# A convolution kernel on one core: one quarter's ninth product moves into the depthwise sums' PSUM banks, and TensorE and ScalarE finish it there

## Chip, cores and metric

The kernel runs on one core of one Trainium2 chip. The metric is the device time of one execution in microseconds (us), as the median of the runs shown.

## What is computed

The input x is 32 images of 64 channels, 56 by 56, in f32. Two blocks follow each other, each on a group-normalised copy of its input (32 groups, so 2 channels to a group) and each added to its input:

```python
x = x + _L0_conv_ref(_gn(x), ...)   # sign, 3x3 depthwise with signs, PReLU, batch norm, sign, 1x1 with signs, PReLU, batch norm, + its input
x = x + _L1_conv_ref(_gn(x), W, b)  # involution

def _L1_conv_ref(x, W, b):
    filters = jnp.einsum('bchw,oc->bohw', x, W) + b[None, :, None, None]
    filters = filters.reshape(B, C, K * K, H, Wd).transpose(0, 1, 3, 4, 2)
    patches = _extract_patches(x)
    return jnp.sum(patches * filters, axis=-1)
```

The second block makes nine filters for every channel and pixel (a 1x1 convolution from 64 to 576 channels), multiplies each with one of the nine shifted copies of the normalised input, and sums the nine products. That second block is where nearly all the time goes.

## The kernel before

**Tiles and quarters.** A tile is two images, which fill the 128 partitions, so there are 16 tiles. A tile is cut into 4 quarters of 14 rows (784 pixels). A quarter has 9 units, one for each place k of the 3x3 window, so a tile has 36 units (unit 0 to unit 35) and the kernel 576.

**One unit.** TensorE makes the filter of place k with 4 matmuls of 64 by 64 in f32 (L451, `unit`); the trace shows 8 rows for them. They fill two PSUM banks of a ring of three slots, `tap_ps`. VectorE adds the bias to it and multiplies by the shifted input `q` in one instruction (L868, `product`), which frees the slot and writes a plane of `prod`. `prod` has 3 buffers of 9 planes, one buffer to a quarter.

**Summing nine planes.** A DMA issued by GpSimd adds planes 0 to 2 onto 3 to 5 (L346, `fold`). Then there are two ways:
- For quarters 1, 2 and 3 of a tile (`POOLED`, tested by `on_pool`), ScalarE adds the mean to plane 8 (L679, seen as L542, `add_mean`) and GpSimd adds planes 6 to 8 onto 3 to 5 (L364), 5 onto 3 (L374), and 3 and 4 into the output buffer `ob` (L385, `final`).
- Quarter 0 of each tile, and all four quarters of the last tile, are "kept": VectorE leaves the ninth product (k = 8) in its PSUM slot and adds it with the mean onto plane 7 in a second instruction (L882, `pair`). GpSimd adds 7 onto 6 (L355, `add_early`), 5 and 6 onto 3 and 4 (L367), and then L385.

**The first block** runs ahead of the second as 4 "jobs" a tile. A job's depthwise convolution (L486, 36 bf16 matmuls in three parts) fills `dw_ps`, a pair of PSUM banks beside the ring. ScalarE takes it out (L570 and L571, seen as L542), a pointwise matmul (L505) and a second pass (L518) use a slot of the ring with a ScalarE pass between them (relu), and VectorE adds the result to `xb` (L842, `x1_sum`), which frees the slot. The sums for the normalisations go between ScalarE (passes over 3136 elements), VectorE (shuffles, L720), GpSimd (powers, L331 and L333) and back to ScalarE, which writes `q`; SyncE copies half of it to `mirror` by DMA (L286).

**What sets the order.** Every engine runs through the same counter of units g, in program order, and waits on semaphores. Step X of a quarter stands at g = 9 x quarter + delay (`FOLD_DELAY`, `OUT_DELAY` and so on), and the steps of the first block at g = 36 x tile + place, from the tables `COURSE` and `EARLY`. So the numbers order an engine's instructions and set no time. `slots_in_turn` hands out the ring's slots and says whose release each unit waits for. VectorE's product k = 3 of a quarter waits for L385 of the quarter three before it.

The end of the last quarter is added by TensorE: `add_to_last` (L460) adds planes 0 to 5 into `dw_ps` with an identity matrix in f32:

```python
for half in range(2):
    mm = pe.matmul(dw_ps[:, half, 0:CH], ident_f32[:], prod[:, g % BUFS, k, half * CH:half * CH + CH],
                   start=(k == 0), stop=(k == PAIR_K - 3))
```

## Time and profile before

| | us |
|---|---|
| median of 3 runs | 739.9 |
| lowest and highest | 738.72, 741.68 |
| the profiled execution's own time | 737.53 |
| its span in the trace | 735.7 |
| mean granted TensorE clock, as a share of full speed | 0.977 |

The profile is of one execution. Busy time of an engine is the time in which one of its instructions ran. In a row of the timeline the first number is the start, the second the duration, both in us. Several like instructions in a row are merged (x3 and so on), and square brackets give the idle time of that engine just before, with what ended it. Consecutive instructions of VectorE overlap by some 0.08 us in these rows, so what one costs is the distance from its start to the next start. PEld is TensorE's weight load. Line numbers are those of the kernel before; all of ScalarE's activations carry the helper's line L542.

### The profile page before, as it was taken

What the parts mean: (1) busy time and instruction counts of PE and PEld (TensorE: products, weight loads), DVE (VectorE), ACT (ScalarE), POOL (GpSimd) and SP (SyncE); (2) the same over time, 40 slices, a digit from 0 to 9 for tenths busy, and PEclk for the clock granted to TensorE, in tenths of its full rate; (3) what the DMA queues carried; (4) which work ended last, traced back from release to release, by engine and by line L of the source; (5) the groups of instructions that cost most, each with busy time, mean ns of one, the idle gap of its engine ahead of it and who ended that gap; (6) DMA issues with size and microseconds to landing.
All of it is one profiled execution on the core that took longest, in us unless ns stands there. A gap on an engine that the chain in (4) does not pass through costs nothing.

```text
span 735.7 us, 18658 instructions
## 1 busy us (share of the span) xinstructions
PE 616.9 (84%) x8001; PEld 251.1 (34%) x8001; DVE 665.5 (90%) x984; ACT 501.5 (68%) x627; POOL 634.6 (86%) x330
## 2 busy tenths in 40 slices
PE   3649899897989888898888889888988889898777
PEld 2324333343333333343333334233333334332213
DVE  4839789999999998999999899999999999999885
ACT  6866896959687695959778695967769595835000
POOL 2003589999999999999999999999999999999996
PEclk9869899999999999999999999999999999999999
DMA  5235596999999798999979798989979896988874
GB/s 205 78 133 103 100 267 150 222 196 219 225 185 267 168 252 172 201 236 207 252 166 262 170 238 191 227 206 186 273 169 253 180 194 147 197 169 184 196 156 125
DMA packets 34279, 142.10 MB, mean 193 GB/s; under 512 B 3348, under 2 KB 11540, under 8 KB 32276
## 3 DMA queue, kind: packets, MB, share of 16 engines
q0 software_dynamic: 17232, 75.87, 56.0%
q1 hardware_dynamic: 16940, 65.03, 26.8%
q8 instruction: 63, 1.03, 0.5%
q14 instruction: 20, 0.16, 0.1%
q10 hardware_dynamic: 24, 0.00, 0.0%
HBM read 26.03 MB, written 25.69 MB: 70 GB/s over the span
## 4 chain that ended last, share of the span: by engine, by line
POOL 33%; DVE 22%; DMA 14%; ACT 13%; PE 12%; issue 5%; SPq 0%; POOLq 0%; DVEq 0%; ACTq 0%
DVE prod L868 16%; POOL prod L364 14%; DMA prod<-prod 11%; POOL ob L385 8%; PE tap_ps L451 7%; POOL prod L374 6%; ACT unused L542 5%; POOL prod L346 4%; DVE xb L842 3%; ACT ab L542 3%; PE dw_ps L486 3%; ACT tap_ps L542 2%; ACT st L542 2%; PE tap_ps L518 2%; DMA mirror<-q 1%
## 5 line engine op out<-in xcount | busy, mean ns | idle before, releaser
L451 PE MATMUL tap_ps<-q,w_t 64*64 64x392 f32 x2304 | 478.4, 507 | 59.6 <-DVE prod L868 38.2
L868 DVE SCALAR_TENSOR_TENSOR prod<-tap_ps,bias,q 128x784 f32<-128x784 f32 x493 | 485.3, 1026 | 31.1 <-PE tap_ps L451 19.8
L451 PE MATMUL tap_ps<-mirror,w_t 64*64 64x392 f32 x2304 | 472.7, 507 | 0.0
L451 PEld LDWEIGHTS tap_ps<-q,w_t 64*64 64x64 f32 x2304 | 147.9, 133 | 276.7 <-DVE prod L868 205.6
L364 POOL TENSOR_TENSOR prod<-prod 128x2352 f32<-128x2352 f32 x45 | 233.8, 5195 | 3.5 <-DMA prod<-prod 3.4
L542 ACT ACTIVATE ab<-dw_ps,col 128x784 bf16<-128x784 f32 x124 | 117.3, 996 | 29.7 <-PE dw_ps L486 29.7
L451 PEld LDWEIGHTS tap_ps<-mirror,w_t 64*64 64x64 f32 x2304 | 136.9, 133 | 1.1 <-issue 1.1
L486 PE MATMUL dw_ps<-signs,dw_diag 64*64 64x392 bf16 x2232 | 131.2, 336 | 6.5 <-issue 3.3
L385 POOL TENSOR_TENSOR ob<-prod 128x784 f32<-128x784 f32 x63 | 125.4, 1991 | 4.3
L346 POOL DMA_DIRECT2D prod<-prod x63 | 79.1, 1256 | 32.3 <-DVE prod L868 31.7
L374 POOL TENSOR_TENSOR prod<-prod 128x784 f32<-128x784 f32 x45 | 103.9, 2308 | 0.0
L486 PEld LDWEIGHTS dw_ps<-signs,dw_diag 64*64 64x64 bf16 x2232 | 71.1, 109 | 86.8 <-issue 75.6
L542 ACT ACTIVATE unused<-xb,st 128x3136 bf16<-128x3136 f32 x31 | 91.4, 2950 | 0.5
L542 ACT ACTIVATE tap_ps<-tap_ps,col 128x784 f32<-128x784 f32 x64 | 61.7, 965 | 39.0 <-PE tap_ps L505 39.0
L542 ACT ACTIVATE st<-st 128x1 f32<-128x1 f32 x176 | 36.4, 238 | 60.7 <-POOL st L333 47.8
L842 DVE SCALAR_TENSOR_TENSOR xb<-tap_ps,st,xb 128x784 f32<-128x784 f32 x64 | 65.9, 1030 | 11.8 <-PE tap_ps L518 10.6
L367 POOL TENSOR_TENSOR prod<-prod 128x1568 f32<-128x1568 f32 x18 | 71.1, 3949 | 0.1
L868 DVE SCALAR_TENSOR_TENSOR prod<-tap_ps,st,q 128x784 f32<-128x784 f32 x64 | 65.7, 1026 | 1.4 <-PE tap_ps L451 0.5
L542 ACT ACTIVATE q<-xb,st 128x1568 f32<-128x1568 f32 x32 | 52.6, 1693 | 0.5
L331 POOL TENSOR_SCALAR st<-st 128x1 f32<-128x1 f32 x32 | 9.4, 295 | 44.8 <-DVE st L720 43.5
L542 ACT ACTIVATE signs<-xb,st 128x3136 bf16<-128x3136 f32 (+5 forms) x20 | 47.5, 2389 | 0.5
L542 ACT ACTIVATE prod<-prod,st 128x784 f32<-128x784 f32 x45 | 42.2, 937 | 7.0 <-DVE prod L868 7.0
(118 smaller groups left out, 378.9 us busy)
## 6 DMA issues: line engine op xcount, KB each, us to landing
prod<-prod POOLq DMA_DIRECT2D x63, 1176.0 KB, 10.5
out_dram<-ob SPq DMA_DIRECT2D x31, 784.0 KB, 5.9
xb<-in_x_dram SPq DMA_DIRECT2D x15, 1568.0 KB, 10.4
mirror<-q SPq DMA_DIRECT2D x64, 203.0 KB, 5.1
xb<-in_x_dram SPq DMA_DIRECT2D x2, 784.0 KB, 5.8
out_dram<-ob SPq DMA_DIRECT2D x2, 392.0 KB, 2.4
prod<-in_L_conv_W_dram SPq DMA_DIRECT2D x1, 288.0 KB
prod<-in_L_conv_pw_weight_dram SPq DMA_DIRECT2D x1, 32.0 KB
```

What stands on the lines that cost most here:

```text
L331: pool.tensor_scalar(s_(t, var), s_(t, own), s_(t, other), EPS * N_GROUP, ALU.add, ALU.add).then_inc(var_done, 1)
L346: pool.dma_start(prod[:, g % BUFS, 3:6, :], prod[:, g % BUFS, 0:3, :], accum_op=ALU.add, max_dma_last_dim=6 * QP).then_inc(folded[g % BUFS ...
L364: pool.tensor_tensor(pr[:, 3:6, :], pr[:, 3:6, :], pr[:, 6:9, :], ALU.add).then_inc(summed_wide, 1)
L367: pool.tensor_tensor(pr[:, 3:5, :], pr[:, 3:5, :], pr[:, 5:7, :], ALU.add).then_inc(summed_wide, 1)
L374: pool.tensor_tensor(pr[3], pr[3], pr[5], ALU.add).then_inc(summed35, 1)
L385: pool.tensor_tensor(ob[:, qq, :], pr[3], pr[4], ALU.add).then_inc(summed, 1)
L451: mm = pe.matmul(rows3(tap_ps[to, slot, side, 0:CH]), w_t[own, k, :], moving, start=True, stop=True)
L486: mm = pe.matmul(rows3(banks[to, image, 0:CH]), dw_diag[own, k, own], signs[own, t.par, first:first + ROWS, dx:dx + WD], start=(k == 0), s ...
L518: mm = pe.matmul(tap_ps[to, slot, chunk, 0:CH], pw_n[own, own], ab[own, j % 2, n, image, :], start=False, stop=(n == 1), skip_group_check= ...
L542: return nc.scalar.activation(o, i, f, **kw)
L842: v.scalar_tensor_tensor(xj, tap_ps[:, slot, :, 0:CH], s_(t, RATIO), xj, ALU.mult, ALU.add, accum_out=sums[:, t.par, j:j + 1]).then_inc(x1 ...
L868: v.scalar_tensor_tensor(place.rearrange("p j (a b) -> p j a b", b=WD), psum.rearrange("p j (a b) -> p j a b", b=WD), s_(t, B4) if k == 4 ...
```

## The change

A third way to sum a quarter is added, tested by `in_banks`. It holds for quarter 3 of the tiles 0 to 14 (`SUMMED`) and for quarters 0 and 1 of the last tile (`SUMMED_LAST`). VectorE writes the ninth product into `dw_ps` instead of plane 8. TensorE adds planes 7 and 6 onto it there, by two calls of `add_in_banks` that stand at the units 10 and 11 after the quarter's first, which are units 1 and 2 of the next quarter. ScalarE takes the sum out with the mean into plane 6 (`take_from_banks`), and GpSimd goes on with L367 (5 and 6 onto 3 and 4) and L385. VectorE's `pair` and GpSimd's `add_early` are left out for these quarters. GpSimd's own way now has quarters 0, 1 and 2. Kept are only quarters 2 and 3 of the last tile. New waits guard `dw_ps`: the ninth product waits until ScalarE has emptied it (`ab_done`), and the next depthwise job waits for `take_from_banks`. The order tables are also changed, and the delays: the fold is issued two units later, `final` three.

```diff
+        def in_banks(g):
+            return g % QUARTERS in (SUMMED if g < (TILES - 1) * QUARTERS else SUMMED_LAST)
+        def is_kept(g):
+            return not on_pool(g) and not in_banks(g)
...
-                if not on_pool(g):
+                if is_kept(g):
                     pool.wait_ge(paired, kept(g))
                     pool.tensor_tensor(pr[6], pr[6], pr[7], ALU.add).then_inc(summed67, 1)
...
+            def add_in_banks(t, qq, k):
+                g = quarter(t, qq)
+                pe.wait_ge(prod_done, KK * (g + 1))
+                for half in range(2):
+                    mm = pe.matmul(dw_ps[:, half, 0:CH], ident_f32[:], prod[:, g % BUFS, k, half * CH:half * CH + CH],
+                                   start=False, stop=(k == 6), skip_group_check=True)
+                if k == 6:
+                    mm.then_inc(banks_added, 1)
...
                         wait(pe, ab_done, j - 1 if t.first else t.count(JOBS, j))
+                        wait(pe, mean_added, banks_with_mean(g))
...
+                for k, delay in ((7, BANK_DELAY), (6, BANK_DELAY + 1)):
+                    for t, qq in quarters(g, delay):
+                        if in_banks(quarter(t, qq)):
+                            add_in_banks(t, qq, k)
...
+            def take_from_banks(t, qq):
+                g = quarter(t, qq)
+                if in_banks(g):
+                    act.wait_ge(banks_added, banked(g))
+                    acts(prod[:, g % BUFS, 6, :].rearrange("p (j n) -> p j n", j=2), dw_ps[:, :, 0:CH], ACT.Identity,
+                         bias=s_(t, MEAN1)).then_inc(mean_added, 1)
...
+                elif k == PAIR_K and in_banks(g):
+                    dve.wait_ge(ab_done, convolved(g))
+                    wait(dve, mean_added, with_mean(g) - 1)
+                    place = dw_ps[:, :, 0:CH]
...
             def pair(t, qq):
                 g = quarter(t, qq)
-                if on_pool(g):
+                if not is_kept(g):
                     return
...
- 'job1': -46,
+ 'job1': -44,
...
- 'var0': -63,
+ 'var0': -65,
...
- 'inverse': -8,
+ 'inverse': -10,
...
-FOLD_DELAY = 4
+FOLD_DELAY = 6
-MEAN_DELAY = 12
+MEAN_DELAY = 10
-POOLED = 1, 2, 3
-OUT_DELAY = 25
+POOLED = 0, 1, 2
+SUMMED = 3,
+SUMMED_LAST = 0, 1
+BANK_DELAY = 10
+TAKE_DELAY = 14
+OUT_DELAY = 28
```

How the instructions move. TensorE at the start of a tile, in the changed kernel, from unit 1 of a tile in the middle (L479 is the filter matmul of `unit`, L487 the new adds; one L487 row is one matmul on one bank). In this place the kernel before has the L451 rows alone, one unit after the other.

```order
L479 MATMUL tap_ps<-q,w_t 64x392 [waits prod_done]
L479 MATMUL tap_ps<-mirror,w_t 64x392 x2
L479 MATMUL tap_ps<-q,w_t 64x392
L487 MATMUL dw_ps<-prod,ident_f 128x392 [waits prod_done]
L487 MATMUL dw_ps<-prod,ident_f 128x392
L479 MATMUL tap_ps<-q,w_t 64x392 [waits x1_done]
L479 MATMUL tap_ps<-mirror,w_t 64x392 x2
L479 MATMUL tap_ps<-q,w_t 64x392
L487 MATMUL dw_ps<-prod,ident_f 128x392 [waits prod_done]
L487 MATMUL dw_ps<-prod,ident_f 128x392
L479 MATMUL tap_ps<-q,w_t 64x392 [waits prod_done]
```

Two adds now stand between the filters of units 1 and 2 and of units 2 and 3.

GpSimd over half a tile, before: L364, L374 and L385 are one quarter's sums on GpSimd, L346 the fold's issue, L355 and L367 the kept quarter's.

```order
L331 TENSOR_SCALAR st<-st 128x1 [waits shuffled_var0]
L333 TENSOR_TENSOR st<-st,minus_half 128x1 [waits var0_done]
L364 TENSOR_TENSOR prod<-prod 128x2352 [waits mean_added,folded0]
L346 DMA prod<-prod 128x2x1176 [waits prod_done]
L374 TENSOR_TENSOR prod<-prod 128x784 [waits summed_wide]
L355 TENSOR_TENSOR prod<-prod 128x784 [waits paired]
L385 TENSOR_TENSOR ob<-prod 128x784 [waits summed35,stored1]
L367 TENSOR_TENSOR prod<-prod 128x1568 [waits summed67,folded1]
```

GpSimd in the changed kernel, in the matching stretch of a tile (L371 is the fold's issue, L395 the sum of two planes, L389 that of three, L413 `final`):

```order
L371 DMA prod<-prod 128x2x1176 [waits prod_done]
L356 TENSOR_SCALAR st<-st 128x1 [waits shuffled_var0]
L358 TENSOR_TENSOR st<-st,minus_half 128x1 [waits var0_done]
L413 TENSOR_TENSOR ob<-prod 128x784 [waits summed35,stored1]
L395 TENSOR_TENSOR prod<-prod 128x1568 [waits mean_added,folded0]
L371 DMA prod<-prod 128x2x1176 [waits prod_done]
L413 TENSOR_TENSOR ob<-prod 128x784 [waits summed_wide,stored1]
L389 TENSOR_TENSOR prod<-prod 128x2352 [waits mean_added,folded1]
```

The instruction L355 is gone, and between the issue of a quarter's fold and the first sum that needs it stand fewer instructions.

## Rows read from the trace of the kernel before

**Rows 1.** The page's first part: busy us and share of the span, by engine.

```profile
PE 616.9 (84%) x8001; PEld 251.1 (34%) x8001; DVE 665.5 (90%) x984; ACT 501.5 (68%) x627; POOL 634.6 (86%) x330
```

**Rows 2.** Timeline of VectorE over two tiles: start, us, instruction, [idle before, releaser].

```profile
485.69 1.02 DVE L868 SCALAR_TENSOR_TENSOR prod<-tap_ps,bias,q 128x784 f32<-128x784 f32 x1
486.63 1.02 DVE L882 SCALAR_TENSOR_TENSOR prod<-tap_ps,st,prod 128x784 f32<-128x784 f32 x1
487.58 0.01 DVE L720 LOAD_MASK_SELECT st<-st  x1
...
492.31 1.03 DVE L842 SCALAR_TENSOR_TENSOR xb<-tap_ps,st,xb 128x784 f32<-128x784 f32 x1 [0.65 <-PE tap_ps L518]
...
502.23 1.03 DVE L868 SCALAR_TENSOR_TENSOR prod<-tap_ps,bias,q 128x784 f32<-128x784 f32 x1 [0.94 <-POOL ob L385]
...
510.98 0.15 DVE L848 RECIPROCAL st<-st 128x1 f32<-128x1 f32 x1
...
515.40 1.03 DVE L868 SCALAR_TENSOR_TENSOR prod<-tap_ps,bias,q 128x784 f32<-128x784 f32 x1 [0.47 <-PE tap_ps L451]
...
534.19 1.03 DVE L842 SCALAR_TENSOR_TENSOR xb<-tap_ps,st,xb 128x784 f32<-128x784 f32 x1 [0.30 <-PE tap_ps L518]
...
543.64 1.03 DVE L868 SCALAR_TENSOR_TENSOR prod<-tap_ps,bias,q 128x784 f32<-128x784 f32 x1 [0.46 <-POOL ob L385]
...
550.03 1.03 DVE L842 SCALAR_TENSOR_TENSOR xb<-tap_ps,st,xb 128x784 f32<-128x784 f32 x1 [0.43 <-PE tap_ps L518]
...
552.88 0.15 DVE L848 RECIPROCAL st<-st 128x1 f32<-128x1 f32 x1
```

**Rows 3.** Timeline of GpSimd from one L367 to the next.

```profile
459.20 3.96 POOL L367 TENSOR_TENSOR prod<-prod 128x1568 f32<-128x1568 f32 x1
...
464.99 0.29 POOL L331 TENSOR_SCALAR st<-st 128x1 f32<-128x1 f32 x1 [0.67 <-DVE st L720]
...
473.35 1.24 POOL L346 DMA_DIRECT2D prod<-prod  x1 [0.43 <-DVE prod L868]
...
490.36 5.19 POOL L364 TENSOR_TENSOR prod<-prod 128x2352 f32<-128x2352 f32 x1 [0.63 <-DMA prod<-prod]
...
498.10 2.29 POOL L355 TENSOR_TENSOR prod<-prod 128x784 f32<-128x784 f32 x1
499.92 2.28 POOL L385 TENSOR_TENSOR ob<-prod 128x784 f32<-128x784 f32 x1
501.75 3.93 POOL L367 TENSOR_TENSOR prod<-prod 128x1568 f32<-128x1568 f32 x1
```

**Rows 4.** VectorE's waits: waiting line, releaser, total us, times, longest.

```profile
DVE prod L868 <- POOL ob L385: 9.8, 14, 2.2
```

**Rows 5.** Timeline of TensorE at the pair of Rows 2.

```profile
486.76 0.54 PE L451 MATMUL tap_ps<-q,w_t 64*64 64x392 f32 x1 [0.61 <-DVE prod L868]
```

**Rows 6.** Timeline of the last quarter: VectorE, and TensorE's adds into dw_ps.

```profile
717.33 2.91 DVE L868 SCALAR_TENSOR_TENSOR prod<-tap_ps,bias,q 128x784 f32<-128x784 f32 x3
...
718.28 1.58 PE L460 MATMUL dw_ps<-prod,ident_f 128*128 128x392 f32 x4
...
719.80 0.54 PE L451 MATMUL tap_ps<-q,w_t 64*64 64x392 f32 x1
...
720.62 1.58 PE L460 MATMUL dw_ps<-prod,ident_f 128*128 128x392 f32 x4
720.76 1.03 DVE L868 SCALAR_TENSOR_TENSOR prod<-tap_ps,st,q 128x784 f32<-128x784 f32 x1 [0.52 <-PE tap_ps L451]
...
723.09 1.03 DVE L868 SCALAR_TENSOR_TENSOR prod<-tap_ps,bias,q 128x784 f32<-128x784 f32 x1 [1.30 <-PE tap_ps L451]
```

**Rows 7.** Timeline of ScalarE in the first tile of Rows 2.

```profile
489.76 0.30 ACT L542 ACTIVATE st<-st 128x1 f32<-128x1 f32 x2 [2.98 <-POOL st L333]
```

**Rows 8.** Timeline of VectorE in a tile in which it never waits for GpSimd.

```profile
129.12 0.01 DVE L720 LOAD_MASK_SELECT st<-st  x1 [0.45 <-ACT unused L542]
...
130.64 1.03 DVE L842 SCALAR_TENSOR_TENSOR xb<-tap_ps,st,xb 128x784 f32<-128x784 f32 x1 [0.43 <-PE tap_ps L518]
```

**Rows 9.** Timeline of VectorE in the last tile.

```profile
709.37 1.03 DVE L868 SCALAR_TENSOR_TENSOR prod<-tap_ps,bias,q 128x784 f32<-128x784 f32 x1 [2.25 <-POOL ob L385]
```

More of the change, by code:

```diff
@@ L197, in on_pool, with banked, with_mean @@
             return g % QUARTERS in POOLED and g < (TILES - 1) * QUARTERS
+        def in_banks(g):
+            return g % QUARTERS in (SUMMED if g < (TILES - 1) * QUARTERS else SUMMED_LAST)
+        def is_kept(g):
+            return not on_pool(g) and not in_banks(g)
         def pooled(g):
             return sum(on_pool(n) for n in range(g + 1))
+        def banked(g):
+            return sum(in_banks(n) for n in range(g + 1))
         def kept(g):
-            return g + 1 - pooled(g)
+            return sum(is_kept(n) for n in range(g + 1))
+        def with_mean(g):
+            return pooled(g) + banked(g)
         def planes(g):
@@ L226, in slots_in_turn @@
                 for t, u in taps(g):
-                    if u % KK != PAIR_K or on_pool(g // KK):
+                    if u % KK != PAIR_K or not is_kept(g // KK):
                         freed["tap", g] = len(freed)
                 for t, qq in quarters(g, KK):
-                    if not on_pool(quarter(t, qq)):
+                    if is_kept(quarter(t, qq)):
                         freed["tap", KK * quarter(t, qq) + PAIR_K] = len(freed)
@@ L240, in preact_involution_kernel, with convolved, banks_with_mean @@
         slots = slots_in_turn()
+        def convolved(g):
+            return sum(1 for n in range(-2 * UNITS, KK * g + PAIR_K) for _ in jobs(n, 0))
+        def banks_with_mean(g):
+            used = [n for n in range(TILES * QUARTERS) if in_banks(n) and KK * n + BANK_DELAY <= g]
+            return with_mean(used[-1]) if used else 0
         def rows3(ap):
@@ L362, in add_wide @@
                 if on_pool(g):
-                    pool.wait_ge(mean_added, pooled(g))
+                    pool.wait_ge(mean_added, with_mean(g))
                     pool.tensor_tensor(pr[:, 3:6, :], pr[:, 3:6, :], pr[:, 6:9, :], ALU.add).then_inc(summed_wide, 1)
                 else:
-                    pool.wait_ge(summed67, kept(g))
+                    if in_banks(g):
+                        pool.wait_ge(mean_added, with_mean(g))
+                    else:
+                        pool.wait_ge(summed67, kept(g))
                     pool.tensor_tensor(pr[:, 3:5, :], pr[:, 3:5, :], pr[:, 5:7, :], ALU.add).then_inc(summed_wide, 1)
@@ L429, in wait_slot @@
                     pe.wait_ge(x1_done, n + 1)
-                elif n % KK == PAIR_K and not on_pool(n // KK):
+                elif n % KK == PAIR_K and is_kept(n // KK):
                     pe.wait_ge(paired, kept(n // KK))
@@ L457, in add_to_last @@
                 pe.wait_ge(ab_done, TILES * JOBS)
+                wait(pe, mean_added, with_mean(g))
                 pe.wait_ge(prod_done, KK * g + k + 1)
@@ L463, in add_to_last, with depthwise @@
                     mm.then_inc(last_added, 1)
-            def depthwise(t, j, taps):
+            def depthwise(t, j, taps, g):
                 if t.n < 2 and taps.start == 0:
@@ L530, in _ @@
                             add_to_last(k)
+                for k, delay in ((7, BANK_DELAY), (6, BANK_DELAY + 1)):
+                    for t, qq in quarters(g, delay):
+                        if in_banks(quarter(t, qq)):
+                            add_in_banks(t, qq, k)
                 for part in range(3):
                     for t, j in jobs(g, part):
-                        depthwise(t, j, range(3 * part, 3 * part + 3))
+                        depthwise(t, j, range(3 * part, 3 * part + 3), g)
                 for t, j in jobs(g, PW_DELAY):
@@ L683, in _ @@
                     add_mean(t, qq)
+                for t, qq in quarters(g, TAKE_DELAY):
+                    take_from_banks(t, qq)
                 for t, j in jobs(g, AB_DELAY):
@@ L866, in product @@
                 psum = tap_ps[:, slots["tap", t.count(UNITS, u)][0], :, 0:CH]
-                place = psum if k == PAIR_K and not on_pool(g) else prod[:, g % BUFS, k, :].rearrange("p (j n) -> p j n", j=2)
+                place = prod[:, g % BUFS, k, :].rearrange("p (j n) -> p j n", j=2)
+                if k == PAIR_K and is_kept(g):
+                    place = psum
+                elif k == PAIR_K and in_banks(g):
+                    dve.wait_ge(ab_done, convolved(g))
+                    wait(dve, mean_added, with_mean(g) - 1)
+                    place = dw_ps[:, :, 0:CH]
                 v.scalar_tensor_tensor(
@@ L927 @@
  'sum0': -74,
- 'mean0': -73,
+ 'mean0': -72,
  'sign0': -71,
  'square0': -67,
- 'var0': -63,
+ 'var0': -65,
  'rstd0': -65,
- 'scales0': -61,
+ 'scales0': -60,
  'inv_z': -55,
@@ L941 @@
  'mean1': -16,
- 'square1': -14,
+ 'square1': -15,
  'var1': -11,
@@ L950 @@
     0: {'sum0': -70,
-     'mean0': -100,
-     'sign0': -68,
+     'mean0': -98,
+     'sign0': -69,
      'square0': -67,
      'var0': -66,
-     'rstd0': -66,
+     'rstd0': -63,
      'scales0': -62,
      'inv_z': -60,
-     'ratio': -60,
+     'ratio': -59,
      'job0': -65,
@@ L965 @@
      'square1': -47,
-     'var1': -45,
+     'var1': -44,
      'rstd1': -49,
-     'q0': -44,
+     'q0': -47,
      'q1': -43,
-     'inverse': -44},
+     'inverse': -41},
  1: {'sum0': -100,
@@ L977 @@
      'scales0': -78,
-     'inv_z': -36,
-     'ratio': -35,
-     'job0': -37,
-     'job1': -29,
+     'inv_z': -37,
+     'ratio': -33,
+     'job0': -39,
+     'job1': -31,
      'job2': -24,
@@ L990 @@
      'q1': -7,
-     'inverse': -5},
+     'inverse': -6},
  2: {'sum0': -60,
-     'mean0': -59,
+     'mean0': -58,
      'sign0': -58,
-     'square0': -53,
-     'var0': -49,
+     'square0': -54,
+     'var0': -50,
      'rstd0': -51,
-     'scales0': -46,
+     'scales0': -47,
      'inv_z': -46,
-     'ratio': -45,
+     'ratio': -43,
      'job0': -42,
-     'job1': -37,
-     'job2': -31,
+     'job1': -32,
+     'job2': -28,
      'job3': -25},
@@ L1010 @@
  'copy_w': -45,
- 'signs_rest': -43,
- 'square_0': -57,
+ 'signs_rest': -45,
+ 'square_0': -59,
  'square_1': -53,
```

5 lines of the change are left out of this document (3 added, 2 removed).

## The prediction

> **What bounds the kernel now.** I read the page's busy times first. VectorE is busy 90% of the span, GpSimd 86%, TensorE 84%, ScalarE 68% [rows 1]. No engine is full, and two are near it, so the shares don't decide. What decides is the length of each engine's loop over one tile, against the time that a tile takes.
>
> One tile takes 41.9 us: from one reciprocal L848 to the next, 510.98 to 552.88, the distance is 41.90 us [rows 2]. GpSimd's loop comes from its timeline. From one L367 to the next are 42.55 us, of which it waited 0.67, 0.43 and 0.63 us, so its own work is 40.8 us a tile [rows 3]. VectorE's timeline over the same stretch shows products 0.94 to 0.95 us apart, and six waits in two tiles: 0.65, 0.94, 0.47, 0.30, 0.46 and 0.43 us, 3.25 together [rows 2]. Two of the six end with GpSimd's L385, and there are 14 such waits in the run, 9.8 us in all [rows 4]. Consecutive instructions overlap by about 0.08 us and a wait breaks that too, so six waits cost 3.25 + 0.48 = 3.7 us, or 1.87 us a tile. VectorE's own work is then 41.9 - 1.9 = 40.0 us. So **VectorE and GpSimd pace the kernel together**. TensorE follows VectorE through the ring: at the pair it stands idle for 0.61 us until VectorE frees a slot [rows 5]. That idle time is the slack into which the change puts work.
>
> **The change, part by part.**
>
> *Removed from VectorE:* the pair. It costs the distance to the next start, 487.58 - 486.63 = 0.95 us [rows 2]. 19 quarters had one and 2 keep it: 17 x 0.95 = 16.1 us, all on VectorE's own line.
>
> *Removed from GpSimd:* L355, 499.92 - 498.10 = 1.82 us in each of the 17 quarters [rows 3]. Its work falls from 40.8 to 39.0 us a tile. That shortens nothing by itself; it can only end VectorE's waits for L385.
>
> *Added to TensorE:* two calls of the add for each of 17 quarters. The last quarter of the kernel before makes the same call, with the same shapes, in the same alternation with filters [rows 6]. The add runs from 718.28 to the next filter's start at 719.80, so it takes 1.52 us; filter and change-over take 720.62 - 719.80 = 0.82 us; a filter is of use to VectorE 720.76 - 719.80 = 0.96 us after its first matmul. A freed slot is refilled from 1.07 us after the start of the product that frees it (486.76 against 485.69) [rows 2, 5]. With three slots VectorE comes back to a slot after 3 x 0.945 = 2.84 us, and 1.07 + 0.96 = 2.03 us are needed, so TensorE may be late by only 0.8 us.
>
> Now step by step at the start of a tile, from the start of the sum L842 that the new order places ahead of unit 0. Product 35 started at -0.95, so the filter of unit 1 starts at 0.12. The first add, which waits for that same product, runs from 0.94 to 2.46. The filter of unit 2 starts at 2.46 and is ready at 3.42. VectorE, after the sum (0.96), product 0, a shuffle (0.06) and product 1, wants it at 2.91: it waits 0.51 us. The second add runs from 3.28 to 4.80, the filter of unit 3 is ready at 5.76, and VectorE wants it at 4.37: 1.39 us. Unit 4 comes in time (6.42 for 6.71). Together **1.90 us**, 15 times: 28.5 us. The two quarters of the last tile have no sum beside them and are like the rows of the last quarter, whose waits of 0.52 and 1.30 cost 1.98 us with the overlap [rows 6]: 4.0 us. The adds cost 32.5 us in all. The bounds are nothing, if the ring hides both, and 2 x (1.52 + 0.15) = 3.3 us a place, if it hides none. I take the walk, since it repeats the waits of the rows.
>
> The row's price against a page: four matmul rows on 2 x 392 columns took 1.52 us. The Trainium skill (FP8 and Floating Point Precision, TensorE Precision Notes) has true FP32 as four passes through the array; at 2.4 GHz that is an estimate of 4 x 784 / 2.4 = 1.31 us. By it both waits shrink by 0.21 us, a place costs 1.5, and the sum ends near 740. No row bears the lower figure out.
>
> *Moved:* the relu before the pointwise's second pass now stands ahead of ScalarE's scales in its queue. Before, ScalarE sat 2.98 us until GpSimd's L333 came [rows 7], and the sum L842 behind it waited 0.65 and 0.30 us [rows 2]. I leave 0.1 of that. The waits for L385 go, since GpSimd gains 1.8 us a tile and its work between the fold that waits for product 5 and `final` is shorter by an L374. What is late next shows in a tile without such a wait: VectorE loses 0.45 us at the shuffle and 0.43 us at the sum [rows 8], with the overlap 1.04 us, as the chain of squares, shuffle and relu has its own length. The reciprocal, two units earlier, adds about 0.1. So 1.25 us of waits stay instead of 1.87: -0.62 us in each of the 12 full tiles in the middle, -7.4 us. The 2.25 us for L385 in the last tile [rows 9] go too: -2.3.
>
> *At nothing:* ScalarE's 17 new passes, one a tile, on an engine that is idle 32% of the span [rows 1]. It can start at 4.8 and the next depthwise job wants the banks at about 7.5, so it is covered unless ScalarE is in a long pass; then up to 1 us a tile shows. The ninth product into PSUM instead of SBUF: the kernel has written it to PSUM in the kept quarters all along, at the same distance.
>
> *The sum:* -16.1 + 32.5 - 7.4 - 2.3 = +6.7 us on the profiled execution's 737.5 us, 744.2. The median of the runs is 2.4 us above that execution, so **746.5 us**, slower by 0.9%.
>
> **The rivals.**
>
> *A, no change.* The pause of 1.9 us at a tile's start gives ScalarE and GpSimd time, and waits that I kept shrink by half (0.5 us in 12 tiles), or a place costs 1.5 us. For it: the chains behind them run on while VectorE stands. Against it: the chain behind the waits of 0.45 and 0.43 us begins at a sum in the middle of the tile, after the pause. 746.5 - 6 = 740.5 us.
>
> *B, faster.* The adds are hidden: TensorE is further ahead at a tile's start than the walk has it. The sum turns when a place costs under (16.1 + 7.4 + 2.3) / 17 = 1.52 us. With nothing left of it the time is 739.9 - 25.8 = 714. GpSimd's loop stops it earlier, by the mechanism of C, at about 732. I put it at 725. Against it: the add and the next filter wait for the same product, so TensorE cannot be ahead there.
>
> *C, slower than forecast.* GpSimd becomes the bound again by the fold's landing. The fold issued at 473.35 was waited for until 490.36, 17.0 us, with 16.4 us of work between [rows 3]. In the new order one L374 stands no longer between; at an L355's 1.82 us that leaves 14.6, a wait of 2.4 us. GpSimd's loop is then 39.0 + 2.4 = 41.4, with its 0.67 us for the shuffle 42.1, beside VectorE's 40.0 - 0.95 + 1.25 + 1.90 = 42.2. Two equal loops that lean on each other lose more than either: at 0.7 us a tile, 755 us. It decides if folds take over 17 us. The Trainium skill (Trainium Kernel Development and Optimization, Key Constraints) says that transfers of all queues interleave on the same 16 DMA engines; the landing just named, beside the tile's other transfers, fits.
>
> *D, the change doesn't do what it says:* excluded by the order of instructions, where L355 and the pair are gone.
>
> **How the numbers follow.** The forecast has 0.45, A 0.27, B 0.13, C 0.15. A measurement of this kernel can tell about 0.5% from no change, 736.2 to 743.6 us. B is faster, and of A 0.05: 0.18. The rest of A and 0.03 of the forecast are the same: 0.25. What is left is slower: 0.57. The range of 8 in 10 leaves out B and the upper third of C: 735 to 756. The forecast's own range is 743 to 751.
>
> **What would show it.** In the profile after, a full tile should take 42.2 us. VectorE should wait for TensorE's filter twice at each tile's start, 0.4 to 0.5 and 1.3 us, with nearly all its waits for L385 gone, and GpSimd should stand idle 2 to 3 us a tile. The adds should take 1.5 us a call. It is wrong if these two waits are missing or add up to under 1.4 us, or if VectorE still waits for GpSimd.

## The result and the profile after

The changed kernel takes **755.69 us** (median of 4 runs, 752.07 to 757.84), the kernel before 740.59 us in the same comparison. The ratio is 1.0202, with a 95% interval of 1.0153 to 1.025: it is slower by 2.0%. The forecast was 746.5 us in a range of 735 to 756. The direction held, and the range by 0.3 us; the size did not: +15 us instead of +6.6. A ratio leaves out runs that are over 1.5% above the fastest of the same kernel, which concerns only two of the four of experiment 1. The profiled execution is the one of 757.84 us, with a span of 755.9 us.

The page of the changed kernel (its busy times, the first line of its chain of waits, and two of its costliest groups; L479 is the filter matmul, L487 the new add, L371 the fold's issue):

```profile
PE 663.8 (88%) x8137; PEld 276.9 (37%) x8137; DVE 652.5 (86%) x967; ACT 519.0 (69%) x644; POOL 604.2 (80%) x313
...
PE 53%; DVE 21%; ACT 16%; DMA 6%; issue 2%; SPq 1%; POOL 1%; DVEq 0%; POOLq 0%; ACTq 0%
...
L371 POOL DMA_DIRECT2D prod<-prod x63 | 76.6, 1216 | 74.3 <-DVE prod L928 72.7
...
L487 PE MATMUL dw_ps<-prod,ident_f 128*128 128x392 f32 x136 | 54.7, 526 | 0.1
```

Against [rows 1] VectorE fell from 90% to 86% and GpSimd from 86% to 80%, while TensorE rose from 84% to 88%. Half of the chain is now TensorE's. GpSimd has spare time: it waited 72.7 us at the fold's issue for VectorE's products, where it had waited 31.7 in the kernel before (15 us of either are one wait at the start).

VectorE's waits in the changed kernel (total, times, longest one, in us; L928 is the product, L774 the shuffle, L902 the reciprocal):

```profile
DVE prod L928 <- PE tap_ps L479: 53.6, 80, 2.4
DVE st L774 <- ACT unused L586: 9.2, 14, 1.2
DVE st L902 <- ACT st L586: 8.0, 16, 1.4
```

There is no wait for GpSimd's final add left in the list, where 14 of them had cost 9.8 us [rows 4]. What stands in their place is the first line, 53.6 us for the filters. VectorE's timeline over one tile of the changed kernel says where:

```profile
358.57 1.02 DVE L896 SCALAR_TENSOR_TENSOR xb<-tap_ps,st,xb 128x784 f32<-128x784 f32 x1
...
360.54 1.02 DVE L928 SCALAR_TENSOR_TENSOR prod<-tap_ps,bias,q 128x784 f32<-128x784 f32 x1
362.01 1.03 DVE L928 SCALAR_TENSOR_TENSOR prod<-tap_ps,bias,q 128x784 f32<-128x784 f32 x1 [0.44 <-PE tap_ps L479]
364.41 1.03 DVE L928 SCALAR_TENSOR_TENSOR prod<-tap_ps,bias,q 128x784 f32<-128x784 f32 x1 [1.37 <-PE tap_ps L479]
...
374.15 1.03 DVE L928 SCALAR_TENSOR_TENSOR prod<-tap_ps,st,q 128x784 f32<-128x784 f32 x1 [0.16 <-PE tap_ps L479]
...
389.41 0.01 DVE L774 LOAD_MASK_SELECT st<-st  x1 [0.62 <-ACT unused L586]
...
390.88 0.16 DVE L902 RECIPROCAL st<-st 128x1 f32<-128x1 f32 x1 [0.38 <-ACT st L586]
```

The two waits at the tile's start, 0.44 and 1.37 us, are those of the walk (0.51 and 1.39). On TensorE's timeline the second add starts at 361.87 and the next filter at 363.38, 1.51 us later, which is the 1.52 of [rows 6]:

```profile
361.87 1.58 PE L487 MATMUL dw_ps<-prod,ident_f 128*128 128x392 f32 x4
363.38 0.54 PE L479 MATMUL tap_ps<-q,w_t 64*64 64x392 f32 x1
```

So far the mechanism is the one forecast. The length of the tiles shows what was not. From one reciprocal L902 to the next the changed kernel takes 42.01 us (348.87 to 390.88), then 43.67 (to 434.55), 42.19 (to 476.74), 43.55 (to 520.29), and so on: short tiles of 42.0 to 42.2, as forecast (42.2), and long ones of 43.6 to 44.1. TensorE's timeline where a long tile starts (its reciprocal is at 606.17; L545 and L558 are the two passes of the pointwise matmul):

```profile
603.59 0.49 PE L479 MATMUL tap_ps<-mirror,w_t 64*64 64x392 f32 x2
603.61 0.49 PE L479 MATMUL tap_ps<-q,w_t 64*64 64x392 f32 x1
605.58 0.53 PE L558 MATMUL tap_ps<-ab,pw_a_sg 64*64 64x392 bf16 x4 [1.49 <-ACT tap_ps L586]
605.89 0.55 PE L558 MATMUL tap_ps<-ab,pw_b_sg 64*64 64x392 bf16 x4
606.22 0.86 PE L479 MATMUL tap_ps<-q,w_t 64*64 64x392 f32 x1
606.22 0.86 PE L479 MATMUL tap_ps<-mirror,w_t 64*64 64x392 f32 x2
606.23 1.49 PE L479 MATMUL tap_ps<-q,w_t 64*64 64x392 f32 x2
606.88 0.86 PE L479 MATMUL tap_ps<-mirror,w_t 64*64 64x392 f32 x2
```

TensorE stood idle for 1.49 us, until ScalarE's relu let L558 start. Then matmuls of the same shape took 0.86 us in place of 0.49, and the step from one group of them to the next 0.66 in place of 0.33 (a unit has two such steps). The windows of that stretch and of the same place of the tile before, where no fall came (each starts with L558; the columns are the width and each engine's busy us, the granted clock as a share of full speed, the DMA share and GB/s):

```profile
605.60:609.10 3.50, 3.50 (x28) 1.53 (x32) 2.27 (x5) 3.13 (x6) 3.50 (x3) 0.51 1.04 184
563.60:567.10 3.50, 3.50 (x60) 1.99 (x64) 3.12 (x6) 3.12 (x6) 3.50 (x3) 1.00 1.05 185
```

The granted clock is 0.51 of full speed there, the lower of its two levels (1.2 GHz), and TensorE starts 28 matmuls in place of 60. Such stretches lie in seven full tiles of the changed kernel: from 175.6, 260.9, 305.3, 390.6, 475.9, 520.3 and 605.6 us, a little over 3 us each. Each begins between 0.3 us before and 0.7 us after the end of the idle time ahead of L558. The idle time is there in every tile, the fall only in these seven. In the kernel before no full tile in the middle has one. The spread of the changed kernel's runs goes with it roughly: 752.07 us at a mean granted clock of 0.977, 754.48 at 0.969, 756.90 at 0.964, 757.84 at 0.966.

The long tile from 305.19 takes 43.68 - 42.01 = 1.67 us more than a short one, and seven times that is 11.7 us. The profiled execution less these is 757.84 - 11.7 = 746.1 us, against the 744.2 of the sum. Of the 1.9 us that are left most are at the start of the last tile, which lies at the low clock as well (701.2 to 704.6, behind 2.48 us of idle time for the `mirror` transfer): the first add takes 2.35 us there, and VectorE waits 2.09 us for the filter behind it where other tiles have 0.44.

### The profile page after: what moved, and what is told of

Read it like the earlier page. It is cut to its first block, busy times and chain, and to the rows that moved or that the text cites. A ratio compares the mean times of both kernels' runs of the same rounds, so it can differ in the third digit from the quotient of the medians.

```text
span 755.9 us, 18972 instructions
## 1 busy us (share of the span) xinstructions
PE 663.8 (88%) x8137; PEld 276.9 (37%) x8137; DVE 652.5 (86%) x967; ACT 519.0 (69%) x644; POOL 604.2 (80%) x313
## 4 chain that ended last, share of the span: by engine, by line
PE 53%; DVE 21%; ACT 16%; DMA 6%; issue 2%; SPq 1%; POOL 1%; DVEq 0%; POOLq 0%; ACTq 0%
PE tap_ps L479 32%; DVE prod L928 15%; PE dw_ps L526 10%; PE dw_ps L487 7%; ACT unused L586 7%; DMA mirror<-q 5%; ACT ab L586 5%; DVE xb L896 3%; PE tap_ps L558 2%; ACT tap_ps L586 2%; DVE dw_ps L928 2%; ACT st L586 1%; PE dw_ps L499 1%; DMA xb<-in_x_dram 1%; PE tap_ps L545 1%
## 5 line engine op out<-in xcount | busy, mean ns | idle before, releaser
L928 DVE SCALAR_TENSOR_TENSOR prod<-tap_ps,bias,q 128x784 f32<-128x784 f32 x493 | 486.2, 1027 | 52.2 <-PE tap_ps L479 50.9
L479 PE MATMUL tap_ps<-q,w_t 64*64 64x392 f32 x2304 | 475.5, 512 | 38.0 <-DVE prod L928 20.5
L479 PE MATMUL tap_ps<-mirror,w_t 64*64 64x392 f32 x2304 | 470.9, 512 | 0.0
L389 POOL TENSOR_TENSOR prod<-prod 128x2352 f32<-128x2352 f32 x45 | 246.9, 5487 | 0.0
L479 PEld LDWEIGHTS tap_ps<-q,w_t 64*64 64x64 f32 x2304 | 152.5, 135 | 232.8 <-DVE prod L928 140.6
L479 PEld LDWEIGHTS tap_ps<-mirror,w_t 64*64 64x64 f32 x2304 | 141.8, 135 | 1.6 <-issue 1.3
L371 POOL DMA_DIRECT2D prod<-prod x63 | 76.6, 1216 | 74.3 <-DVE prod L928 72.7
L413 POOL TENSOR_TENSOR ob<-prod 128x784 f32<-128x784 f32 x63 | 133.0, 2110 | 0.1
L526 PEld LDWEIGHTS dw_ps<-signs,dw_diag 64*64 64x64 bf16 x2232 | 68.9, 110 | 96.4 <-issue 72.1
L402 POOL TENSOR_TENSOR prod<-prod 128x784 f32<-128x784 f32 x45 | 83.8, 1862 | 3.5
L928 DVE SCALAR_TENSOR_TENSOR prod<-tap_ps,st,q 128x784 f32<-128x784 f32 x64 | 65.8, 1029 | 3.0 <-PE tap_ps L479 2.6
L395 POOL TENSOR_TENSOR prod<-prod 128x1568 f32<-128x1568 f32 x18 | 65.7, 3647 | 1.7 <-DMA prod<-prod 1.6
L487 PE MATMUL dw_ps<-prod,ident_f 128*128 128x392 f32 x136 | 54.7, 526 | 0.1
```

The source lines that it names most:

```text
L371: pool.dma_start(prod[:, g % BUFS, 3:6, :], prod[:, g % BUFS, 0:3, :], accum_op=ALU.add, max_dma_last_dim=6 * QP).then_inc(folded[g % BUFS ...
L389: pool.tensor_tensor(pr[:, 3:6, :], pr[:, 3:6, :], pr[:, 6:9, :], ALU.add).then_inc(summed_wide, 1)
L395: pool.tensor_tensor(pr[:, 3:5, :], pr[:, 3:5, :], pr[:, 5:7, :], ALU.add).then_inc(summed_wide, 1)
L402: pool.tensor_tensor(pr[3], pr[3], pr[5], ALU.add).then_inc(summed35, 1)
L413: pool.tensor_tensor(ob[:, qq, :], pr[3], pr[4], ALU.add).then_inc(summed, 1)
L479: mm = pe.matmul(rows3(tap_ps[to, slot, side, 0:CH]), w_t[own, k, :], moving, start=True, stop=True)
```

## The experiments

All compare with the kernel before on the same chip: 739.3 us there in the first four, 738.2 in the next four and 738.6 in the last three. The table sums them up; "low-clock tiles" counts the full tiles between 100 and 650 us that have a stretch at half clock, in the one profiled execution of each kernel.

| kernel | us | ratio to before, 95% | low-clock tiles |
|---|---|---|---|
| the change | 755.7 | 1.020 (1.015 to 1.025) | 7 |
| 1 job 1 back | 772.6 | 1.038 (1.028 to 1.047) | 11 |
| 2 adds apart | 752.8 | 1.019 (1.015 to 1.022) | 7 |
| 3 both | 769.6 | 1.042 (1.038 to 1.045) | 9 |
| 4 adds on 8 columns | 725.0 | 0.982 (0.979 to 0.985) | 1 |
| 5 orders without adds | 742.9 | 1.006 (1.004 to 1.008) | 4 |
| 6 adds on the orders of before | 787.0 | 1.065 (1.061 to 1.068) | 3 |
| 7 job 1 back, mean later | 749.6 | 1.014 (1.010 to 1.018) | 0 |
| 8 the same, adds apart | 747.4 | 1.011 (1.007 to 1.014) | 0 |
| 9 as 7, fp16 planes | 723.5 | 0.979 (0.977 to 0.981) | 0 |
| 10 the change, fp16 planes | 723.3 | 0.979 (0.977 to 0.981) | 2 |
| 11 as 5, job 1 back, mean later | 741.1 | 1.003 (1.001 to 1.004) | 0 |

### 1. The depthwise part of job 1 where it was

In the kernel before, a depthwise part stood between the filters and L518 (the second pass of the pointwise there), where TensorE idled for 0.6 us at most in the full tiles from 170 us on:

```profile
549.38 0.36 PE L518 MATMUL tap_ps<-ab,pw_a_sg 64*64 64x392 bf16 x4 [0.43 <-ACT tap_ps L542]
```

The change moved that part two units later.

```diff
- 'job1': -44,
+ 'job1': -46,
```

> The changed kernel with one number of its order table put back: job 1 of the first block starts at -46 instead of -44, so that a part of its depthwise convolution again stands in TensorE's queue before the second pointwise pass of job 0, where TensorE of the changed kernel idles 1.49 us. Theory (half clock): in seven of the tiles of the changed kernel TensorE falls to 1.2 GHz for one stretch after that idle time, and each such tile takes 43.7 instead of 42.0 us. With the idle time filled the falls are gone from the full tiles and the median is 743 to 747 us (755.7 less 7 x 1.7). Rival (the longer tiles come from the adds or from late transfers, and the clock only goes along): every second tile stays at 43.7 us and the median is 753 to 757 us.

Measured: 772.58 us, the median of 760.99, 771.84, 773.32 and 774.58; the ratio goes by the two lower ones. A miss to the other side, by 14 us or more in every run. The trace is that of the longest run; experiment 3 has the same edit, and its four runs lie between 767.8 and 769.8. TensorE's idle times in one tile of this kernel:

```profile
353.55 0.36 PE L558 MATMUL tap_ps<-ab,pw_a_sg 64*64 64x392 bf16 x4 [0.98 <-ACT tap_ps L586]
...
360.90 0.36 PE L545 MATMUL tap_ps<-ab,pw_a 64*64 64x392 bf16 x4 [1.79 <-ACT ab L586]
...
362.51 0.54 PE L558 MATMUL tap_ps<-ab,pw_a_sg 64*64 64x392 bf16 x4 [0.42 <-ACT tap_ps L586]
```

The edit did shorten the idle time ahead of the first L558, from 1.49 to 0.98 us; that it isn't back at 0.6 has a second cause, given below with the step that failed. But job 1's own pointwise part came two units earlier too, and ScalarE wasn't ready: its timeline has the mean of quarter 2 (358.04) ahead of that job's prelu (358.88), behind 3.29 us of q. TensorE idled for 1.79 us in its place, and 0.42 more ahead of L558, and there the clock fell (granted clock 0.51 from 362.3 to 365.7), now in nearly every full tile: tiles of 44.4 us. Eleven full tiles had a fall, where the change had seven. The remedy moved the idle time and made it longer. The link from idle time to low clock stood; that the adds or the load do it was as open as before.

### 2. The adds apart

```diff
-                for k, delay in ((7, BANK_DELAY), (6, BANK_DELAY + 1)):
+                for k, delay in ((7, BANK_DELAY), (6, BANK_DELAY + 3)):
```

> The changed kernel with the second add two units later: plane 6 at unit 4 of the next quarter instead of unit 2. Theory (ring slack): an add alone makes TensorE 1.5 us late, of which the ring hides 0.8 us, and two in neighbouring units find the slack gone. Apart, VectorE waits about 0.5 us for each instead of 0.44 and 1.37 us: 17 x 0.85 = 14 us less, a median of 740 to 744 us while the falls of the clock stay. Rival (TensorE is full at a tile's start, so that the wait only moves): waits of 0.4 and 1.3 us as before at another unit, 753 to 757 us.

Measured: 752.83 us, 2.9 less than the change. A miss: it lies by the rival's 753 to 757 us, and the waits came as neither had them. VectorE's timeline at a tile's start:

```profile
405.16 1.98 DVE L928 SCALAR_TENSOR_TENSOR prod<-tap_ps,bias,q 128x784 f32<-128x784 f32 x2 [0.59 <-PE tap_ps L479]
...
408.81 2.92 DVE L928 SCALAR_TENSOR_TENSOR prod<-tap_ps,bias,q 128x784 f32<-128x784 f32 x3 [0.73 <-PE tap_ps L479]
```

The wait for the second add fell from 1.37 to 0.73 us, but the one before it grew to 0.59 and another later in the tile from 0.16 to 0.27. Between the two adds TensorE can't catch up: VectorE takes a product each 0.95 us, and a filter with its add takes more than two of them. Seven tiles kept their fall of the clock.

### 3. Both

> Both edits: job 1 at -46 and the second add at unit 4. Theory (ring slack and half clock, two costs that add up): 755.7 - 12 - 14, a median of 728 to 732 us, 1.2% faster than the kernel before. Rival (GpSimd's loop over a tile with the fold's landing, about 42 us, is the next bound): the gains do not add up, no less than 739 us, and VectorE waits for L385's counterpart again.

Measured: 769.59 us, the edits of 1 and 2 together. A miss for the reason of the first: TensorE idles for 1.77 us ahead of job 1's L545 in every full tile, and nine of them had a fall. What the adds apart give here isn't clear, since the runs of the first lie between 761.0 and 774.6.

### 4. Adds on eight columns

The two planes are added on 8 of 392 columns, so most of them is left out of the sum; every instruction and wait stays.

```diff
-                    mm = pe.matmul(dw_ps[:, half, 0:CH], ident_f32[:], prod[:, g % BUFS, k, half * CH:half * CH + CH],
+                    mm = pe.matmul(dw_ps[:, half, 0:8], ident_f32[:], prod[:, g % BUFS, k, half * CH:half * CH + 8],
```

> The changed kernel with every add cut to 8 columns of each bank; all waits and semaphores stay. Left out: planes 6 and 7 are added on 8 of 392 columns only. Theory (ring slack): the two waits at a tile's start vanish, 17 x 1.9 = 32 us less, a median of 722 to 728 us, and the falls of the clock stay in every second tile. Rival (GpSimd's loop takes over, as it was the other pacer before): 738 to 742 us with VectorE waiting for GpSimd.

Measured: 725.03 us, a hit: 30.7 us less than the change, where the prediction put the adds at 32.5. VectorE waited 17.4 us for filters in place of 53.6:

```profile
DVE prod L928 <- PE tap_ps L479: 17.4, 29, 2.4
```

Its waits for GpSimd's final add were 1.3 us in 7 times. So GpSimd is hardly a bound even 30 us lower, and rival C has no place.

But the 30.7 us are not the adds alone. One full tile had the low clock here and seven in the change, and at 1.67 us a tile that is an estimate of 10 of them. A full tile without the low clock takes 40.65 us (338.89 to 379.54) against the change's 42.01, so the adds cost 1.36 us a tile, less than the 1.97 us of their waits. The rest is in waits that only this kernel's tiles have:

```profile
357.65 0.01 DVE L774 LOAD_MASK_SELECT st<-st  x1 [0.33 <-ACT unused L586]
...
361.77 1.03 DVE L928 SCALAR_TENSOR_TENSOR prod<-tap_ps,bias,q 128x784 f32<-128x784 f32 x1 [0.17 <-POOL ob L413]
```

In the change VectorE's pause for the adds covers them. That is the mechanism of rival A, at other waits than it named.

### 5. The orders without the adds

```diff
-SUMMED = 3,
-SUMMED_LAST = 0, 1
+SUMMED = ()
+SUMMED_LAST = ()
```

> The changed kernel's orders and delays without its adds in the banks: quarter 3 (and quarters 0 and 1 of the last tile) are summed by VectorE's pair and GpSimd again. Theory (adds 1.9 us a place, pairs 0.95, and the half clock comes from where the orders let TensorE wait): 755.7 less 17 times (1.9 less 0.95) is 739.5, with the half-clock stretches of the change still in about half of the full tiles: 737 to 743 us. Rival 1 (the adds bring the clock down): no stretches, 726 to 731 us. Rival 2 (GpSimd needs the lighter load that the change gives it, with these delays): VectorE waits at L413 or for prod buffers, 743 us or more.

Quarter 3 is then a kept one, where the kernel before has quarter 0.

Measured: 742.92 us, inside the theory's range and at the edge of rival 2's. Without a single add in the banks four full tiles had a stretch at half clock, and TensorE's timeline has the same 1.49 us ahead of L558:

```profile
385.56 0.36 PE L558 MATMUL tap_ps<-ab,pw_a_sg 64*64 64x392 bf16 x4 [1.49 <-ACT tap_ps L586]
```

This refutes that only the adds bring the clock down: it falls with the new orders alone. The waits of rival 2 came too:

```profile
DVE prod L928 <- POOL ob L413: 13.8, 9, 1.6
```

They are [rows 4] again, with a little more in them (9.8 us there). So the lighter load on GpSimd, and not the new orders, had ended these waits in the change.

The same trace shows that a fall of the clock has no fixed price. A tile without one takes 42.35 us here, with a wait of 1.55 us for L413 in it. A tile with one has waits for filters and no wait for L413, and takes 42.62:

```profile
343.54 0.16 DVE L902 RECIPROCAL st<-st 128x1 f32<-128x1 f32 x1 [0.38 <-ACT st L586]
...
386.16 0.17 DVE L902 RECIPROCAL st<-st 128x1 f32<-128x1 f32 x1 [0.38 <-ACT st L586]
```

A fall costs 0.27 us a tile here, against 1.67 in the change, since VectorE would have waited for GpSimd in the same tile.

### 6. The adds on the orders of before

The changed kernel with the places of `mean0`, `var0`, `scales0`, `job1`, `square1` and `inverse` and the delays of fold, mean and output as in the kernel before. The tables for the first tiles stay those of the change.

```diff
- 'scales0': -60,
- 'job1': -44,
+ 'scales0': -61,
+ 'job1': -46,
...
-FOLD_DELAY = 6
-MEAN_DELAY = 10
-OUT_DELAY = 28
+FOLD_DELAY = 4
+MEAN_DELAY = 12
+OUT_DELAY = 25
```

> The adds in the banks with the kernel before's orders of parts and its delays for fold, mean and output. Theory (the same prices, the clock as in the kernel before, none of the waits term of -7.4 us): 739.3 less 16.1 and plus 32.5 is 755.7: 752 to 758 us, with no half-clock stretch in the full tiles. Rival (the adds bring the clock down by themselves): stretches in 7 or more full tiles, 765 us or more.

Measured: 786.95 us, 31 us above what the terms give. A miss of both theories: only three full tiles had the low clock, though TensorE idled for 2.0 us in eleven of them. What took the time is on ScalarE's and TensorE's timelines:

```profile
432.00 0.30 ACT L586 ACTIVATE st<-st 128x1 f32<-128x1 f32 x2 [2.63 <-POOL st L358]
```

```profile
434.80 0.36 PE L558 MATMUL tap_ps<-ab,pw_a_sg 64*64 64x392 bf16 x4 [2.02 <-ACT tap_ps L586]
```

The scales stand ahead of the relu in ScalarE's queue and wait 2.63 us for GpSimd, then TensorE idles 2.02 us for the relu, and VectorE waits 1.99 us at its sum behind L558. This is the chain of [rows 7] of the kernel before, which cost VectorE only 0.65 and 0.30 us there. VectorE's waits for L558 are 32.5 us in all, against 4.7 in the change:

```profile
DVE xb L896 <- PE tap_ps L558: 32.5, 28, 2.0
```

So the term for the moved steps, -7.4 us, isn't a sum that stands by itself. With the adds the new orders are worth 787.0 - 755.7 = 31 us; without them the fifth run, whose kept quarter is another too, is 4 to 5 us slower than the kernel before.

### 7. Job 1 back, and the means behind it

The repair that the first run's trace asks for.

```diff
- 'job1': -44,
+ 'job1': -46,
...
-MEAN_DELAY = 10
+MEAN_DELAY = 12
```

> The first experiment again (the depthwise part of job 1 two units earlier), with ScalarE's mean steps two units later as well (delay 12 instead of 10), as in the kernel before: the mean of quarter 2 then stands behind the job's prelu in ScalarE's program and not ahead of it. Theory (the half clock follows the stretches of 1.5 to 1.8 us in which TensorE waits for ScalarE at a pointwise part): the 1.79 us ahead of job 1's pointwise part become 1 us or less, the 0.98 ahead of L558 stay, no stretch is long enough, and the full tiles lose their half-clock stretches: tiles of about 42.0 us, 742 to 747 us in all. Rival (the adds, or the load on the engine as a whole, bring the clock down, wherever it waits): half-clock stretches of 3.4 us stay in the full tiles, tiles of 43.7 us or more, 755 to 772 us.

Measured: 749.56 us. The mechanism came as the theory has it, the time 2.6 us above its range. TensorE's idle times in one tile:

```profile
429.86 0.36 PE L558 MATMUL tap_ps<-ab,pw_a_sg 64*64 64x392 bf16 x4 [0.98 <-ACT tap_ps L586]
...
436.37 0.36 PE L545 MATMUL tap_ps<-ab,pw_a 64*64 64x392 bf16 x4 [0.94 <-DVE prod L928]
...
437.98 0.36 PE L558 MATMUL tap_ps<-ab,pw_a_sg 64*64 64x392 bf16 x4 [0.42 <-ACT tap_ps L586]
```

The 1.79 us are gone. Windows over the same place of a tile in this kernel and in that of the first run, which differ in the place of ScalarE's mean steps alone; each starts 0.2 us before job 1's L558, the first in the seventh run, the second in the first:

```profile
437.80:441.20 3.40, 3.19 (x40) 1.16 (x40) 3.40 (x5) 2.96 (x3) 3.40 (x3) 1.00 1.02 297
```

```profile
362.30:365.70 3.40, 3.19 (x24) 1.36 (x28) 2.87 (x4) 2.98 (x3) 3.40 (x4) 0.51 1.14 366
```

No tile between 100 and 650 us had a stretch at half clock, with all the adds in place. Every tile takes 42.4 us (the shuffle of the tile's start at 399.93 and at 442.36). That is 0.4 us above the change's short tiles, since the start's wait is 0.58 in place of 0.44 and a new one of 0.31 us stands at the moved job. The books of the profiled executions close to 1 us: 757.84 - 11.7 + 13 x 0.42 = 751.6 us against 750.69.

### 8. The same, with the adds apart

> The edit of the run before it, and the second add two units later than in the change, so that a filter matmul group stands between the adds. Theory: no half-clock stretches in full tiles, and VectorE's waits at a tile's start fall from 0.44, 1.37 and 0.16 us to about 0.5, 0.73 and 0.27: 13 to 16 tiles by 0.3 to 0.5 us less than without this, 737 to 743 us, level with the kernel before or a little behind. Rival (load brings the clock down): 752 to 770 us.

Measured: 747.44 us, 4.4 us above the theory's range. The edit of the second run gave 2.1 us here. It is the best of the kernels with f32 planes in the banks, and still 1.1% behind the kernel before.

### 11. The orders without the adds, job 1 back and the means behind it

The edit of the seventh run on the fifth run's kernel.

> The fifth experiment's kernel (the change's orders, no adds in the banks), with job 1 two units earlier and the mean steps two later. Theory (half clock follows the 1.49 us idle ahead of L558): the 4 half-clock stretches of the full tiles go, 6.7 us less than 742.9, and GpSimd's 13.8 us of waits at L413 stay or grow by a part of it: 736 to 741 us, level with the kernel before. Rival (the stretches come from the order as a whole): 742 us or more, with 4 or more stretches.

Measured: 741.11 us. The four low-clock stretches went, but only 1.8 us of time, where the theory had put 6.7 on them; the time lies 0.1 us above its range. The waits for GpSimd came in every tile (15.3 us in 13 times), and every tile takes 42.3 us, with the 0.3 us wait at the moved job in it and 1.25 for L413 in place of 1.55. So GpSimd paced this kernel as it paced the fifth, and the falls had cost little there: 4 x 0.27 = 1.1 us.

### 10 and 9. The two planes in fp16

Experiment 4 puts 30 us on what the adds' columns cost, some 10 us of low clock included. Planes 6 and 7 of a summed quarter are read by TensorE alone, so VectorE can write them as fp16; their values are then rounded to fp16, and the other seven planes stay f32. The tenth run does that to the change and nothing else:

```diff
+        def half_plane(g, k):
+            return prod[:, g % BUFS, k, :].bitcast(FP16)[:, 0:QP]
...
-                    mm = pe.matmul(dw_ps[:, half, 0:CH], ident_f32[:], prod[:, g % BUFS, k, half * CH:half * CH + CH],
+                    mm = pe.matmul(dw_ps[:, half, 0:CH], ident[:], half_plane(g, k)[:, half * CH:half * CH + CH],
...
+                if k in (6, 7) and in_banks(g):
+                    place = half_plane(g, k).rearrange("p (j n) -> p j n", j=2)
```

> The change itself, nothing moved, with the same two planes in fp16. Theory (passes): 755.7 less 22 to 31 is 725 to 734 us, with the 1.49 us idle ahead of L558 and its half-clock stretches in some full tiles, so 4 to 12 us behind the run before it. Rival 1 (the adds' load helps to bring the clock down): no stretches, as far down as the run before. Rival 2 (passes are not the cost): 742 us or more.

Measured: 723.27 us, 32.4 less than the change and 2.1% under the kernel before (0.9787, 0.9767 to 0.9807). That is 1.7 us below the theory's range. VectorE's timeline at a tile's start:

```profile
389.69 1.97 DVE L933 SCALAR_TENSOR_TENSOR prod<-tap_ps,bias,q 128x784 f32<-128x784 f32 x2
391.82 1.03 DVE L933 SCALAR_TENSOR_TENSOR prod<-tap_ps,bias,q 128x784 f32<-128x784 f32 x1 [0.16 <-PE tap_ps L482]
```

Where 0.44 and 1.37 us were, one wait of 0.16 is left in this tile, and in others (459.31 to 499.96) none; such a tile takes 40.65 us, as with the adds on eight columns. Two full tiles had the low clock. So 5 falls fewer, 8 us, are in the 32.4 us as well.

The ninth run has the edit on the seventh run's kernel:

> The kernel of the seventh experiment (job 1 two units earlier, mean steps two later, no half clock in full tiles), with planes 6 and 7 of the summed quarters written by VectorE as fp16 and added by TensorE with the fp16 identity: these two planes are rounded to fp16, the other seven stay f32. Theory (an add costs its passes over 784 columns: f32 takes 1.52 us, 16 bit a third of it or less): VectorE's waits of 0.58 and 1.37 us at a tile's start go, or stay under 0.3 each, and 17 places give back 1.3 to 1.8 us each: 749.6 less 22 to 31 is 719 to 728 us, under the kernel before. Rival (what an add costs is mostly the wait for the product and the change of matmul shape, not the passes): 738 us or more.

Measured: 723.48 us, inside its range and the same as the tenth, which had been expected 4 to 12 us behind. It has no low clock in any full tile, but its tiles take 40.94 us against 40.65, which is worth about what the two falls cost. Its TensorE timeline has the price of an add:

```profile
431.13 0.51 PE L490 MATMUL dw_ps<-prod,ident 128*128 128x392 f16 x2
431.57 0.54 PE L482 MATMUL tap_ps<-q,w_t 64*64 64x392 f32 x1
```

From 431.13 to 431.57 are 0.44 us, where an f32 add took 1.51. The group has two records in place of four. The Trainium skill (FP8 and Floating Point Precision, TensorE Precision Notes) gives true FP32 four passes through the array, and names no number of passes for 16-bit operands; the trace has a ratio of 1.51 / 0.44 = 3.4 for the whole add, change of shape included.

## Why the prediction was right in its sign and wrong in its size

- *The step that failed:* the moved step was costed on ScalarE, VectorE and GpSimd, and never on TensorE. Ahead of the second pointwise pass TensorE's idle time grew from 0.6 us at most to 1.49. Half of that is the depthwise part of job 1, two units later: with it back the first run has 0.98. The other half is ScalarE: the relu stands behind a pass over 3136 elements and starts 2.31 us after the pointwise matmul (386.96 to 389.27), where it was 1.76 in the kernel before (546.61 to 548.37). As idle time on an engine with slack it counted as nothing. What it did was bring the granted clock to its lower level for seven tiles, 1.67 us each: 11.7 of the missing 13.6 us of the profiled execution. With the adds in place the falls end when the idle times are 1 us or less (11 full tiles in the first run, none in the seventh, which differ in the mean steps alone), and without the adds too (four in the fifth, none in the eleventh). The sum had no term for the clock, and no rival had one either.
- *The adds, +32.5 us:* the waits are right, the time is not. Two waits of 0.44 and 1.37 us, with 0.16 later in the tile, stand where the walk had 0.51 and 1.39, and a call takes 1.51 us (1.52 forecast). But the fourth run puts the price at 30.7 us less some 10 for the low clock, about 20.7, or 1.36 us a tile: the pause for the adds covers other waits, as rival A had it.
- *The savings, 25.8 us (the pairs, the moved steps and L385 in the last tile):* too large by nearly as much. The fourth run, which has the savings and hardly any of the adds, is 14.3 us below the kernel before, or 16 without its one fall. A tile goes from 41.9 to 40.65 us, 1.25 in place of the 1.57 forecast; that is 3.8 us over the 12 tiles in the middle, and the rest wasn't traced. That the sum still gave 744.2 us, against 746.1 without the falls, and a tile of 42.2 against 42.0, is in part luck: two terms of 10 to 12 us too much each cancel.
- *The pairs, -16.1 us:* no run takes them out alone. The fifth, which has the pairs and not the adds, is 12.8 us below the change. The terms give 17 x (1.97 - 0.95) = 17.3 us, less 13.8 of waits for GpSimd, plus 5.0 for three falls fewer, 8.5 in all (the falls count in full here, since the 13.8 us of waits lie in the nine tiles without one). Another 3.5 us are an estimate from the overlap of 0.08 us that each wait breaks, as VectorE has 44 waits more in the change; 0.8 us stay open.
- *The waits that stay, 1.25 us a tile:* right in size, at other places than forecast: the rows have 0.62 at the shuffle and 0.38 at the reciprocal, where the prediction had 0.45 at the shuffle and 0.43 at the sum L842. The term was set down as one that stands by itself. The fifth run shows that the waits for GpSimd's final add end with the load that the adds take from it, and the sixth that the orders then save far more than 7.4 us. The two halves of the change need each other.
- *Rival C* named 755 us, nearly the time measured, by another mechanism. VectorE has no wait for GpSimd left, and GpSimd idles 3.2 us in a short tile (2 to 3 forecast), so it was not this. The upper end of the stated range, 756 us, stood for part of this rival: that the range held is luck, while the forecast's own range, 743 to 751, did not hold.
- *Rival B:* with fp16 planes the adds' waits are gone and the change takes 723 us, near the 725 that B was given, though not by what it named. Its turning point of 1.52 us a place rests on the 25.8 us; with the 16 measured it is 16 / 17 = 0.94.

What stays open is why the same 1.49 us of idle time brought the clock down in seven tiles and not in the others, and in seven, one, four and two in the runs 2, 4, 5 and 10. Longer idle times aren't enough of an answer: 1.79 us brought a fall in nearly every tile of the first run, and 2.0 us in three of eleven in the sixth. So a share of the adds in how often it falls isn't excluded: with full f32 adds it was seven tiles, with thin ones one. The runs show only that no fall came in the full tiles of the four kernels whose idle times there are 1 us or less (runs 7, 8, 9 and 11), nor in those of the kernel before.

## What to carry to other kernels

Cost a moved step on every engine that it leaves a hole in, the one with slack too: on TensorE a hole of 1.5 to 1.8 us can cost as much again in the matmuls behind it, so look for idle stretches there beside the granted clock of the windows that follow. What it costs depends on who would wait otherwise: 1.67 us a tile in the change, 0.27 in the fifth run. When TensorE is given an addition, the type of what it adds is the price: 1.5 us for f32 and 0.44 for fp16 here, which turned 2% slower into 2% faster, at the price of rounding two of nine planes. A table of orders and the load that it was tuned for are one thing; the same orders were worth 31 us with the adds, and without them they gave nothing.

## What the runs showed of the hardware that was not expected

The granted clock fell to its lower level on a TensorE that was busy 88% of the span, behind an idle time of only 1.49 us, in some tiles and not in others of the same length and order. Executions of one program differ by it: the first run's kernel took 760.99 us at a mean granted clock of 0.979, and 771.84 at 0.964. A repair that ended all of these stretches gave back 6 us, where they had cost 11.7 in the profiled execution, since each tile then took 0.4 us longer.
